# Self-attention in a one-core four-layer kernel: the PSUM ring of three banks used one bank at a time, the period of the head groups written anew

## The reference

```python
att = jnp.einsum('bhqd,bhkd->bhqk', q, k) * scale
att = jnp.where(causal[None, None], att, -jnp.inf)
y = jnp.einsum('bhqk,bhkd->bhqd', jax.nn.softmax(att, axis=-1), v)
...
a = jax.nn.softmax(jnp.einsum('bhsd,bhtd->bhst', q, k) * D ** (-0.5), axis=-1)
if causal:
    a = a * mask
o = jnp.einsum('bhst,bhtd->bhsd', a, v)
x_out = x + o @ li1_w + li1_b
```

## Time and profile before

| | us |
|---|---|
| median of 3 runs | 3694.36 (3685.41 to 3697.6) |
| the profiled execution's own time | 3683.47 |
| its span | 3681.7 |
| first self attention (causal) in the trace | about 42.8 to 308.4 |
| second self attention (non-causal) in the trace | about 1016.2 to 1265.0 |

### The profile page before, as it was taken

One profiled execution on the slowest core, in us unless ns is written; L12 is line 12 of the kernel. 1 busy time (PEld: TensorE's weight loads), 2 busy tenths in 40 slices (PEclk: granted clock), 3 DMA queues, 4 the chain that ended last, 5 costly groups with the idle time before them and its releaser, 6 DMA issues. The chain is left out here.

```text
span 3681.7 us, 81479 instructions
## 1 busy us (share of the span) xinstructions
PE 3195.9 (87%) x32814; PEld 1692.8 (46%) x32814; DVE 2342.6 (64%) x4405; ACT 1847.4 (50%) x2371; POOL 1360.9 (37%) x910
## 2 busy tenths in 40 slices
PE   6898999999689837999999999986886699999985
PEld 4663333333266534555555555544553233333334
DVE  4556888888656553666555656623434576888877
ACT  2332777777433322555555555542223266777762
POOL 2001111110344351888888888872013311111003
PEclk8997999999899965999999999987887587999987
DMA  4200211110010021000000000001212132211100
GB/s 66 33 2 11 58 36 33 36 36 22 15 32 2 1 54 36 11 2 11 11 9 3 11 11 2 2 1 21 53 45 34 28 65 37 46 38 33 29 2 12
DMA packets 70470, 90.95 MB, mean 25 GB/s; under 512 B 37170, under 2 KB 51026, under 8 KB 70098
## 3 DMA queue, kind: packets, MB, share of 16 engines
q1 hardware_dynamic: 69666, 85.36, 11.4%
q10 hardware_dynamic: 432, 0.39, 0.0%
HBM read 35.09 MB, written 4.33 MB: 11 GB/s over the span
## 5 line engine op out<-in xcount | busy, mean ns | idle before, releaser
L2110 DVE TENSOR_REDUCE mx<-ps 128x2 f32<-128x802 f32 (+1 forms) x1372 | 1020.6, 778 | 240.7 <-PE ps L1989 220.4
L2054 ACT ACTIVATE probs<-ps 128x1024 f32<-128x1024 f32 (+1 forms) x832 | 825.8, 1024 | 196.9 <-PE ps L1974 190.5
L2495 DVE TENSOR_REDUCE mx<-ps 128x1 f32<-128x401 f32 x1024 | 534.4, 570 | 375.7 <-PE ps L2382 371.9
L2540 POOL TENSOR_TENSOR sums<-sums,probs 128x2048 f32<-128x2048 f32 x160 | 724.4, 4528 | 32.0 <-ACT probs L2466 21.0
L2382 PE MATMUL ps<-kt,qt 32*128 32x401 f32 x2048 | 542.8, 554 | 2.2 <-DVE mx L2495 2.0
L2007 PE MATMUL ps<-probs,v_cur 128*9 128x256 f32 x6656 | 543.6, 398 | 0.4 <-ACT probs L2054 0.4
L1989 PE MATMUL ps<-kt,qs 48*128 48x401 bf16 x2048 | 481.1, 361 | 51.6 <-DVE mx L2110 35.9
L2466 ACT ACTIVATE probs<-ps 128x1024 f32<-128x1024 f32 x384 | 383.0, 1023 | 226.5 <-PE ps L2360 223.5
L2360 PE MATMUL ps<-qt,kt 32*128 32x256 f32 (+1 forms) x3328 | 443.1, 383 | 0.0
L2151 POOL CAST max_pieces<-negm 128x8 bf16<-128x8 f32 x64 | 12.1, 189 | 1070.8 <-DVE negm L2115 1070.8
L1974 PE MATMUL ps<-qs,kt 50*128 50x256 bf16 (+1 forms) x3328 | 382.4, 285 | 11.2 <-DMA qs<-max_rows 9.3
(11 more groups left out here) (395 smaller groups left out, 4303.4 us busy)
## 6 DMA issues: line engine op xcount, KB each, us to landing
kt<-k SPq DMA_DIRECT2D x680, 50.0 KB
ctx_s<-in_ctx_t SPq DMA_DIRECT2D x16, 400.2 KB, 4.6
ctx_s<-ctx_norm_t SPq DMA_DIRECT2D x16, 400.2 KB
kt<-k SPq DMA_DIRECT2D x24, 200.1 KB
ctx_norm_t<-ctx_norm_t SPq DMA_DIRECT2D x8, 400.2 KB, 3.7
ctx_a<-in_ctx_t SPq DMA_DIRECT2D x8, 400.2 KB
ctx_b<-in_ctx_t SPq DMA_DIRECT2D x8, 400.2 KB
qs<-q SPq DMA_DIRECT2D x12, 256.0 KB
```

The costliest lines, as they stand in the source:

```text
L2054: act.activation(pr[0:m, u % 3, :], pair[0:m].rearrange("p a n -> p (a n)"), ACT.Exp, scale=scale).then_inc(s_free, 1)
L2110: dve.tensor_reduce(mx[:, n % 2, i0:i0 + count], src, AX_X, ALU.max).then_inc(freed(step), 1)
L2495: dve.tensor_reduce(mx[:, n % 2, at:at + 1], rbank(step)[:, 0:CH], AX_X, ALU.max).then_inc(ring_free, 1)
L2540: pool.tensor_tensor(o, o, p, ALU.add).then_inc(added, 1)
```

## The change

The plan now has a period of one group, and the ring is three slots of one bank each, handed out in turn, each with a semaphore of its own for full and for free. A max step holds one head instead of three. The projection leaves banks 0 to 3: queries and keys of a group fill one ring bank (`qk`), the values another (`v`), with separate copies on ScalarE. Within the period the denominators and the weighing of the group before come first, then VectorE's take, then the fourth head's max of the next group, the scores, three heads' max of the group after that, `qk`, `neg`, `v`. The scores raise `s_full` once for each of the four heads, and ScalarE waits for all four.

```diff
-    period = [("scores", 0, 0), ("weigh", -1, 2), ("sums", -1, 2), ("neg", 0, 1), ("project", 1, 0), ("take", -1, 2),
-              ("max", 0, 3), ("scores", 0, 1), ("max", 1, 0), ("weigh", 0, 0), ("project", 1, 1), ("neg", 0, 2),
-              ("sums", 0, 0), ("take", 0, 0), ("max", 1, 1), ("scores", 0, 2), ("weigh", 0, 1), ("sums", 0, 1),
-              ("take", 0, 1), ("out", 0, 0), ("out", -1, 1), ("out", -1, 2), ("project", 1, 2), ("neg", 1, 0),
-              ("max", 1, 2)]
...
+    for i in range(-3, SG + 3):
+        steps = [("sums", i - 1, 0), ("weigh", i - 1, 0), ("take", i - 1, 0), ("max", i + 1, 3), ("scores", i, 0),
+                 ("max", i + 2, 0), ("max", i + 2, 1), ("max", i + 2, 2), ("qk", i + 3, 0), ("neg", i + 1, 0),
+                 ("v", i + 3, 0)]
+        plan += [step for step in steps if 0 <= step[1] < SG]
+        if 0 <= i - 2 < SG and (i - 2) % 4 == 3:
+            plan.append(("out", (i - 2) // 4, 0))
...
+        def rbank(step):
+            return k.ps[:, 4 + ring[step] % 3, :]
...
+        def wait_bank(eng, step):
+            wait(eng, free(step), ring[step] // 3)
...
                 elif kind == "max":
-                    wait_drained(pe, ("project", heads(n)[-1][0]))
-                    wait(pe, ring_free, ring[step])
+                    wait_consumed(pe, ("qk", n, 0))
+                    wait_bank(pe, step)
                     for t in range(QT):
                         nk = P * (t + 1) if causal else S
-                        for u, (g, j) in enumerate(heads(n)):
-                            ins = pe.matmul(rbanks[:, u, S * t:S * t + nk], q[rows(j), g % 4, P * t:P * t + P],
-                                            key[rows(j), g % 4, 0:nk], start=(t == 0),
-                                            stop=(t == QT - 1 and not causal))
+                        ins = pe.matmul(rbank(step)[:, S * t:S * t + nk], q[rows(u), n % 4, P * t:P * t + P],
+                                        key[rows(u), n % 4, 0:nk], start=(t == 0), stop=(t == QT - 1 and not causal))
...
                     if causal:
-                        dve.tensor_reduce(mx[:, at:at + count, 0], rbanks[:, 0:count, 0:P], AX_X, ALU.max,
-                                          negate=True).then_inc(half, 1)
-                        dve.tensor_reduce(mx[:, at:at + count, 1], rbanks[:, 0:count, S:2 * S], AX_X, ALU.max,
-                                          negate=True).then_inc(ring_free, 1)
+                        dve.tensor_reduce(mx[:, at, 0:1], rbank(step)[:, 0:P], AX_X, ALU.max, negate=True).then_inc(half, 1)
+                        dve.tensor_reduce(mx[:, at, 1:2], rbank(step)[:, S:2 * S], AX_X, ALU.max,
+                                          negate=True).then_inc(free(step), 1)
```

More of the change, by code:

```diff
@@ L741, in _ @@
                 pe.matmul(obank[:, 0:C], k.ones[:], row[:], start=True, stop=True).then_inc(row_full, 1)
-            for kind, n in plan:
-                step = (kind, n)
+            for step in plan:
+                kind, n, u = step
                 b, a = n // 4, n % 4
[L745 to L748, removed]
+                if kind == "qk":
+                    wait_bank(pe, step)
+                    pe.matmul(rbank(step)[:, 0:S], wq[:, P * a:P * a + P], xq[:, S * b:S * b + S], start=True, stop=True)
+                    pe.matmul(rbank(step)[:, S:2 * S], wk[:, P * a:P * a + P], xk[:, S * b:S * b + S], start=True,
+                              stop=True).then_inc(full(step), 1)
+                elif kind == "v":
+                    wait_bank(pe, step)
@@ L762, in _ @@
                     if causal:
                         for t in range(QT):
[L764 to L768, removed]
+                            at = S * t + P * t
+                            ins = pe.matmul(rbank(step)[:, at:at + P], k.identb[:], hide[:], start=False,
+                                            stop=(t == QT - 1))
@@ L789, in _ @@
                                             start=False, stop=(t == 1 and not causal))
+                            if t == 1 and not causal:
+                                ins.then_inc(s_full, 1)
                     if causal:
@@ L919, in _ @@
             pool.wait_ge(masks, 3)
-            done = 0
-            for kind, n in plan:
+            for step in plan:
+                kind, n, u = step
                 if kind == "max":
-                    while done < SG and (4 * done + 3) // 3 == n:
-                        g = done
-                        wait_consumed(pool, ("max", n))
+                    if u == 3:
+                        g = n
+                        wait_consumed(pool, step)
                         if g >= 2:
-                            wait_ring(pool, ("neg", g - 2))
-                        at = 4 * g % 24
+                            wait_ring(pool, ("neg", g - 2, 0))
+                        at = 4 * (g % 6)
                         neg = mx[:, at:at + 4, :].rearrange("p j q -> p q j")
```

131 lines of the change are left out of this document (63 added, 68 removed).

## The result

The changed kernel takes 3824.23 us (median of 4 runs, 3817.45 to 3834.46) against 3689.89 (3684.84 to 3697.6) for the kernel before on the same chip: 1.0365 times as long, interval 1.0331 to 1.0398. I had forecast 3770 with 3738 to 3812: slower, as said, but by 134 us and not by 80.

The account below looks back on a forecast made before the run. TensorE was taken to bound the causal stage (busy 46.4 of 50 us), a chain over GpSimd's masking the changed non-causal one. Causal +45 and non-causal +35 gave +80: 3763 or 3774, taken as 3770, range 3738 to 3812.

Parts of the forecast that it names:

- The one-head max step: Causal stage, TensorE: one head's max with its masks costs 1.07 us, four 4.28 a group instead of 1.73, +2.55.
- No bank waits in the causal stage: Causal stage: no bank wait lands on TensorE; old waits of 0.95 us a group go, leaving 9.3 against 7.69.
- Causal +45: Causal stage: +1.6 us a group over 31 intervals, 50 us, less 5 for the last two intervals.
- Non-causal: Non-causal stage: chain through GpSimd's masking sets a 7.8 us floor, 9.4 with output; 8.35 against 7.22 a group, +35.
- more: Rival, both stages: bank waits of 0.6 us a group, 38 us, about 3810; with in-order heads and dear waits, chance 0.20.
- in-order part: Non-causal stage: if matmuls keep strict program order, plain periods 7.9, with output 9.9, some 6 us more in all.
- The clock: Rival: a fifth of both stages, some 115 us, at half clock stretches them by about 100, to 3870; chance 0.05.
- Faster: Rival: heads overlap as before, one-head step under 0.67 us; causal -28, non-causal +6, 3672; chance 0.04, half holding 0.02.
- less: Rival: causal as forecast or a little under, non-causal only +10 through a shorter GpSimd chain or hidden max; 3735; chance 0.12.

Follow-up runs that it names:

- old kernel with exchanged loops: The kernel before, with only the order inside a max step changed: one head's matmuls and mask matmuls after the other's; 3829.32 us, 1.0348.
- new kernel without masks: The changed kernel without the mask matmuls in the causal max steps, scores still masked; 3738.54 us, 1.0148.
- spread: The changed kernel with queries and keys between the first and second head's max, the turn between second and third; 3805.01 us, 1.0339.
- four in a row: The changed kernel with the scores ahead of the fourth head's max, so four one-head steps follow each other in both stages; 3916.56 us, 1.0623.
- together: The changed kernel with the first three heads' maxima made side by side once three one-bank slots are free; 3837.71 us, 1.0392.
- second spread run: Causal stage with the new plan, queries and keys and the turn between one-head max steps; non-causal stage as in the kernel before; 3747.98 us, 1.0137.

## Why the prediction missed its range

**The one-head max step: right.** The changed kernel's causal timeline at full clock:

```profile
274.69 0.92 PE L759 MATMUL ps<-qkv 32*128 32x128 f32 x4
275.54 0.28 PE L764 MATMUL ps<-maskb,identb 128*128 128x128 bf16 x2
275.75 0.92 PE L759 MATMUL ps<-qkv 32*128 32x128 f32 x4
276.60 0.29 PE L764 MATMUL ps<-maskb,identb 128*128 128x128 bf16 x2
276.82 0.92 PE L759 MATMUL ps<-qkv 32*128 32x128 f32 x4
...
277.79 0.65 PE L745 MATMUL ps<-xt,wq_pad 128*128 128x256 f32 x2
```

0.85 to the mask and 1.06 or 1.07 to the next step, for 0.86 and 1.07 forecast; before, three heads took 1.30.

**No bank waits in the causal stage: right.** TensorE is busy for 337.67 of 345.00 us. The fourth head's step stands at 272.03 in one period and at 280.85 in the next, 8.82 apart, forecast 8.83 without an output.

**Causal +45: right at full clock** (46.9), wrong in us.

**Non-causal: the chain is right to a few hundredths, the size a little high.** One period, changed:

```profile
1264.83 0.65 PE L826 MATMUL ps<-probs_kept,qkv 128*32 128x128 f32 x16
...
1265.41 0.48 PE L759 MATMUL ps<-qkv 32*128 32x256 f32 x1
...
1265.42 0.49 PE L779 MATMUL ps<-qkv 32*128 32x256 f32 x3
...
1267.74 1.94 ACT L866 ACTIVATE probs<-ps 128x1024 f32<-128x1024 f32 x2 [3.82 <-PE ps L785]
...
1268.59 1.10 PE L759 MATMUL ps<-qkv 32*128 32x256 f32 x4 [0.64 <-DVE mx L884]
...
1269.82 2.50 POOL L956 TENSOR_TENSOR probs_kept<-probs,mask 128x512 f32<-128x512 f32 x2 [0.77 <-ACT probs L866]
```

The exponential starts 2.33 after the fourth head's first matmul (forecast 2.36), the masking 4.41 (4.44), and the third head, held by the fourth head's bank, 3.18 (waiting to 3.15). At full clock, plain periods last 7.84 to 7.87 between VectorE's reciprocals (7.8 forecast), early ones 8.24, those with an output 9.80 (9.4). 28.8 us at full clock for the 35 forecast. Where the 6 went I have not taken apart further. The scores begin 0.01 after the first of the fourth head's matmuls, in free rows: that matmuls pass each other held here too, and with it falls the in-order part of the rival "more". Its other part, waits for banks, is there only in this stage and was in the forecast.

**The clock: the step that failed.** The sum has no term for it; it stood only as a rival. I wrote: "Against: the mean is 1.00 in the window with many gaps, and TensorE will now have fewer", and gave 0.05. TensorE did get fewer gaps, hardly any, and its clock fell. The step was to take gaps for the only thing that lowers the clock. The changed kernel as its clock falls, after some 100 us with hardly a gap:

```profile
186.02 1.43 PE L759 MATMUL ps<-qkv 32*128 32x128 f32 x4
...
187.38 0.39 PE L764 MATMUL ps<-maskb,identb 128*128 128x128 bf16 x2
187.57 1.17 PE L745 MATMUL ps<-xt,wq_pad 128*128 128x256 f32 x2
```

Nothing is waited for, and the step takes 1.55 instead of 1.07, partly at half clock; near the start of the stage, at 53 to 57 us, such steps are 1.90 apart. The clock record has 14 falls within the causal stage. TensorE was idle for 3.1 of the 7 us ahead of the last of them, at 380.8, and for less than 0.1 us in all ahead of each of the other thirteen. In the non-causal stage the picture is less clean: eight falls of 3.4 us each behind 0.7 to 1.1 us of idle time, and one at 1384.4 that gives the stage's last 18 us at half clock; but TensorE is idle there for 34.6 us in all, and was for 34.4 before.

That rival had the amount about right and its price too high: a fifth of both stages, some 115 us, for about 100. In the trace it is 85.1 + 50.2 = 135.3 us against 32.1 before, and the 103 more cost, by the table's differences, 79.8 - 46.9 = 32.9 in the causal stage and 47.5 - 28.8 = 18.7 in the non-causal: 51.6 us. With the 10.5 between, which are not shown to come of the change, that is 62 us. The forecast from the execution's own time was 3763.5, and the changed kernel's span of 3818.9 with 1.8 around it makes 3820.7: 57 more, which is, to 1 us, these 62, less the 6 of the non-causal stage, plus 2 of the causal.

**Faster, and less: no.** The steps did not come closer than 1.06, and the non-causal stage lost 28.8 at full clock, not 10. **More:** 3810 and the result are near each other only by chance, since TensorE does not wait for banks in the causal stage.

**What is shown and what stays open.** Shown: the surplus is half clock (same code, 0.51 us for each us); in the causal stage it comes with the one-head steps and their masks (old kernel with exchanged loops 175.8 us, new kernel without masks 28.5), and without idle gaps ahead of the falls; the order of the same matmuls changes it (spread, from 140 us on, 3.4 us or none, against 37.5 and 66; four in a row 128.1); more dense work elsewhere in the period does not cure it (116.8). Open: which property of such a run of steps makes the clock fall, what sets the clock at a stage's start, what lowered it in the changed non-causal stage and ahead of it, and why the non-causal stages of "together" and "four in a row" fell to 0.76 and 0.79. In those two, TensorE's idle time had doubled, so gaps are not excluded as the cause there.

## What to carry to other kernels

Matmuls of one row group are cheap only beside their neighbours: a matmul over all rows behind each of them makes every one pay its whole chain (1.07 us for one head where three had 1.30), so first ask whether the full-array matmul can be left out or collected behind all the heads. When steps of few rows come to stand in a row, don't count the clock as safe because TensorE has no gaps: multiply each stage's length by its granted clock in both traces, and compare those products apart from the lengths. A change that takes away waits can give their time back this way. And look where a surplus lies before giving it a cause: the unchanged stretch between the stages varied from 704.6 to 728.1 us between the traces.

## What was not expected of the hardware

TensorE was busy for 50.00 of 50.00 us at a granted clock of 0.86, and in another order of the same steps, in the same window, at 1.00. The Trainium skill, "TensorE: Matmul & The Clock Gate", section "HAM oscillation — how this bites in real kernels", puts falls of the clock down to idle gaps of TensorE. In kind the traces agree for the causal stages of the kernel before, of the new one without masks and of the spread order, whose falls come with 2.1 to 5.5 us of idle time close by, with one exception of 3.4 us at 364.8 in the second spread run. Thirteen of the changed kernel's 14 falls there have no such gap.
